# Linear attention stage: keys and queries of the next group ahead, expert weights of the preceding group on ScalarE

## The reference, cut to what matters

```
qkv = einsum('oc,bcn->bon', W_qkv, x_ext)   # x_ext: 256 tokens and 16 memory columns
q = softmax(q, over the 16 of a head) * SCALE
k = softmax(k, over the tokens and memory)
context = einsum('bhdn,bhen->bhde', k, v)
out = einsum('bhde,bhdn->bhen', context, q)
y = W_out @ out + b_out
y = (y - mean) / sqrt(var + EPS) * ln_g + ln_b
x = x + y
```

## Time and profile before

| what | value |
| --- | --- |
| median of 3 runs | 1226.85 us (1224.17 to 1227.85) |
| profiled execution | 1225.73 us, its span 1223.8 us |
| TensorE busy over the span | 913.3 us, 75% |
| VectorE busy over the span | 743.2 us, 61% |
| ScalarE busy over the span | 629.7 us, 51% |
| GpSimd busy over the span | 275.1 us, 22% |

### The profile page before, as it was taken

The page is one execution under the profiler, slowest core; times in us unless marked ns, Lnnn a source line. Parts: engine busy times, 40 slices in busy tenths (PEclk is TensorE's granted clock), DMA queues, the critical chain, the costliest instruction groups (busy, mean ns, idle before and its releaser), DMA issues. The chain is left out here.

```text
span 1223.8 us, 21857 instructions
## 1 busy us (share of the span) xinstructions
PE 913.3 (75%) x6760; PEld 593.2 (48%) x6760; DVE 743.2 (61%) x1939; ACT 629.7 (51%) x1286; POOL 275.1 (22%) x304
## 2 busy tenths in 40 slices
PE   4778426487878888075889895899675999977297
PEld 2566312377777778064666663333342333324142
DVE  6588769333333333576888887777587444445664
ACT  4444210133333333366888884687584777756253
POOL 2000110555656554232000001011231000015100
PEclk9565655699999899575999997899796999998699
DMA  3221160011010110200101110000100000000000
GB/s 110 66 59 47 32 109 0 19 20 21 18 19 19 19 19 12 80 35 10 53 35 51 51 44 18 1 1 0 53 1 1 1 1 0 0 0 21 1 0 35
DMA packets 25265, 33.05 MB, mean 27 GB/s; under 512 B 11376, under 2 KB 14422, under 8 KB 24814
## 3 DMA queue, kind: packets, MB, share of 16 engines
q1 hardware_dynamic: 20206, 27.50, 7.9%
q0 software_dynamic: 4992, 4.67, 2.0%
HBM read 19.31 MB, written 4.91 MB: 20 GB/s over the span
## 5 line engine op out<-in xcount | busy, mean ns | idle before, releaser
L1673 DVE SCALAR_TENSOR_TENSOR routed_hid_stage<-ps,routed_act_stage 128x512 f32<-128x512 f32 (+1 forms) x117 | 70.4, 602 | 176.7 <-ACT routed_act_stage L1457 139.5
L1746 PE MATMUL ps<-routed_x_stage,w_sb 128*128 128x256 f16 x858 | 122.6, 284 | 41.8 <-ACT routed_x_stage L1465 28.9
L1044 ACT ACTIVATE hid_stage<-ps,b_col_sb 128x512 f32<-128x512 f32 x192 | 122.8, 684 | 47.0 <-PE ps L985 46.8
L1457 ACT ACTIVATE routed_act_stage<-ps 128x512 f32<-128x512 f32 x117 | 70.3, 602 | 135.2 <-PE ps L1746 109.6
L1756 PE MATMUL ps<-w_sb,routed_hid_stage 128*128 x936 | 124.2, 276 | 3.7 <-issue 3.7
L1756 PEld LDWEIGHTS ps<-w_sb,routed_hid_stage 128*128 128x128 f32 x936 | 117.8, 197 | 5.7 <-issue 3.4
L1746 PEld LDWEIGHTS ps<-routed_x_stage,w_sb 128*128 x858 | 85.2, 104 | 60.0 <-issue 46.1
L985 PE MATMUL ps<-x_sb,w_sb 128*128 (+1 forms) x384 | 103.6, 388 | 6.1 <-ACT hid_stage L1044 6.1
L1002 PE MATMUL ps<-hid_stage,w_sb 128*64 128x512 f32 x384 | 105.2, 626 | 0.0
L1510 POOL DMA_INDIRECT routed_got_stage<-expert_rows,take_stage x78 | 80.3, 1029 | 81.7 <-DVE give_stage L1650 58.2
L1518 POOL DMA_INDIRECT expert_out<-routed_rows_stage,give_stage x78 | 78.2, 1002 | 89.9 <-ACT routed_rows_stage L1472 72.1
(11 more groups left out here) (382 smaller groups left out, 1878.4 us busy)
## 6 DMA issues: line engine op xcount, KB each, us to landing
w_stage_sb<-f_w SPq DMA_DIRECT2D x32, 176.0 KB, 3.1
x_sb<-w_sb SPq DMA_DIRECT2D x16, 256.0 KB, 2.4
rt_sb<-vals_stage SPq DMA_DIRECT2D x16, 256.0 KB, 2.3
rel_bias_sb<-bias_bands SPq DMA_DIRECT2D x16, 128.0 KB
w_stage_sb<-f_w SPq DMA_DIRECT2D x14, 128.0 KB, 3.0
w_sb<-f_w SPq DMA_DIRECT2D x1, 1536.0 KB
routed_got_stage<-expert_rows,take_stage POOLq DMA_INDIRECT x78
expert_out<-routed_rows_stage,give_stage POOLq DMA_INDIRECT x78
```

Source lines behind the costliest of these rows:

```text
L1044: nc.scalar.activation(hid[:, n % RING, :], ps[:, n % H_BANKS, :], func, bias=b1_col[:, b:b + 1], scale=UNSCALE).then_inc(h_act, 1)
L1457: nc.scalar.activation(act_h[:, n, :], ps[:, H1 + (q + n) % 2, :], ACT.Silu, scale=UNSCALE).then_inc(h_act, 1)
L1673: last = nc.vector.scalar_tensor_tensor(hid[:, q % 2, n, 0:full], ps[:, H3 + (q + n) % 2, 0:full], UNSCALE, act_h[:, n, 0:full], ALU.mult, ...
L1746: last = nc.tensor.matmul(o, w16[:, part, bass.ds(col, P)], xb[:, q % 2, :], start=(part == 0), stop=(part == 1))
```

## The change

TensorE makes k and q of group g+1 in one piece (`project(0)`, with a semaphore of its own, `queries_ps`), the values of g+1 behind the context in one piece (`project(1)`, `values_ps`), and turns the keys of g+1 (`turn_keys`) ahead of the last product of group g. VectorE takes maxima and subtraction of group g+1 at the head of group g, and so has q of g+1 ready in group g; it no longer copies the turned k, which ScalarE does (L602 of the changed kernel). ScalarE takes the square of group g-2 behind the exponential of q, and scales the weights of group g-1, one chunk behind the square and the other behind the x copy. In the LayerNorm, the bias `ln_b` is added to all of x at once by GpSimd at the head of the stage, the mean's factor is taken into the subtraction, and the multiplications by 1/sigma and `ln_g` become one instruction for each of the four tiles of 64 columns. The factor of the inverse sum goes into `mix`.

```
# ScalarE, group(g, squared=None, halves_of=None, last_group=False)
                         act.wait_ge(q_shifted, g + 1)
                         nc.scalar.activation(q_tok[:, :, :, :], q_tok[:, :, :, :], ACT.Exp,
                                              scale=UNSCALE).then_inc(q_exped, 1)
-                        act.wait_ge(qv_ps, g + 1)
+                        if squared is not None:
+                            square(squared)
+                        if halves_of is not None:
+                            split_high(halves_of, 0)
+                        act.wait_ge(values_ps, g + 1)
                         nc.scalar.activation(v_tok[:, :, :], v_ps, ACT.Copy, scale=UNSCALE).then_inc(v_copied, 1)
                         if not last_group:
                             nc.scalar.copy(x_grp[:, :], x16[:, bass.ds((g + 1) * GTOK, GTOK)]).then_inc(x_copied, 1)
-                        split_high(g, 0)
+                        if halves_of is not None:
+                            split_high(halves_of, 1)
                         act.wait_ge(kt_ps, g + 1)
                         nc.scalar.copy(kt_mem[:, :, :], ps[0:MEM, 4, 0:2 * HID0].rearrange(
-                            "p (b d) -> p b d", b=2)).then_inc(ktm_copied, 1)
-                        if not first:
-                            square(g - 1)
+                            "p (b d) -> p b d", b=2)).then_inc(kt_copied, 1)
+                        nc.scalar.copy(kt[:, :, :], ps[:, 3, :].rearrange(
+                            "p (t d) -> p t d", t=TPG)).then_inc(kt_copied, 1)
                         act.wait_ge(qt_ps, g + 1)
                         nc.scalar.copy(q_ch[:, :], ps[:, 7, :]).then_inc(qt_copied, 1)
-                        split_high(g, 1)
...
+                    group(0)
+                    group(1, halves_of=0)
+                    with act.Fori(2, GROUPS - 1) as g:
+                        group(g, squared=g - 2, halves_of=g - 1)
+                    group(GROUPS - 1, squared=GROUPS - 3, halves_of=GROUPS - 2, last_group=True)
+                    square(GROUPS - 2)
+                    split_high(GROUPS - 1, 0)
+                    split_high(GROUPS - 1, 1)
                     square(GROUPS - 1)
# TensorE
+                    def project(w):
+                        for t in range(TPG):
+                            for part in range(2):
+                                last = nc.tensor.matmul(qv[:, w, t, :], x_grp[:, t * P:(t + 1) * P],
+                                                        qvk16[:, part, w * HID0:(w + 1) * HID0],
+                                                        start=(part == 0), stop=(part == 1))
                         return last
...
# GpSimd
+                    pool.wait_ge(loaded["l0"], want["l0"])
+                    nc.gpsimd.tensor_tensor(x_tok[:, :, :], x_tok[:, :, :],
+                                            ln_rows[:, 2, :].unsqueeze(1).broadcast_to((P, NT, C)),
+                                            ALU.add).then_inc(x_biased, 1)
# VectorE, centre and finish
-                        c.link(nc.vector.tensor_scalar(y_st[:, 0, :], y_st[:, 0, :], 1.0 / C, None, ALU.mult))
-                        nc.vector.tensor_tensor(y, y, wide4(y_st[:, 0, :]), ALU.add).then_inc(y_sq_in, 1)
+                        nc.vector.scalar_tensor_tensor(y, wide4(y_st[:, 0, :]), 1.0 / C, y, ALU.mult,
+                                                       ALU.add).then_inc(y_sq_in, 1)
...
-                        c.link(nc.vector.tensor_tensor(y, y, wide4(y_st[:, 3, :]), ALU.mult))
-                        c.link(nc.vector.tensor_tensor(y, y, rows(1), ALU.mult))
-                        c.link(nc.vector.tensor_tensor(y, y, rows(2), ALU.add))
+                        for t in range(TPG):
+                            last = nc.vector.scalar_tensor_tensor(y[:, t, :], y[:, t, :], y_st[:, 3, t:t + 1],
+                                                                  ln_rows[:, 1, :], ALU.mult, ALU.mult)
+                        c.link(last)
# VectorE, group(g)
+                        if not last_group:
+                            maxima(g + 1)
                         if not first:
-                            variance(g - 1)
-                        split_low(g, 0)
-                        if not first:
-                            finish(g - 1)
+                            centre(g - 1)
+                        if not last_group:
+                            query_sums(g + 1)
                         dve.wait_ge(ctx_ps, g + 1)
                         nc.vector.tensor_tensor(ctx_t[:, :, :], ...
-                        split_low(g, 1)
+                        if not last_group:
+                            query_ready(g + 1)
                         dve.wait_ge(mix_ps, g + 1)
                         ...
+                        if not first:
+                            variance(g - 1)
+                        split_low(g, 0)
+                        if not last_group:
+                            dve.wait_ge(mix_ready, g + 1)
+                            key_inverse(g + 1)
+                        if not first:
+                            finish(g - 1)
+                        split_low(g, 1)
```

More of the change, by code:

```diff
@@ L576, in split_high, with group @@
                                              scale=WEIGHT_SCALE).then_inc(w_high_e, 1)
-                    def group(g, first=False, last_group=False):
+                    def group(g, squared=None, halves_of=None, last_group=False):
                         act.wait_ge(k_max, g + 1)
@@ L622, in keys, with turn_keys @@
                         last.then_inc(k_ps, 1)
-                    def queries_values(tiles):
-                        for t in tiles:
-                            for w in range(2):
-                                for part in range(2):
-                                    last = nc.tensor.matmul(qv[:, w, t, :], x_grp[:, t * P:(t + 1) * P],
-                                                            qvk16[:, part, w * HID0:(w + 1) * HID0],
-                                                            start=(part == 0), stop=(part == 1))
+                    def project(w):
[4 more added lines that the diff above has]
+                                                        start=(part == 0), stop=(part == 1))
                         return last
-                    def group(g, last_group=False):
+                    def turn_keys(g):
                         pe.wait_ge(k_exped, g + 1)
@@ L736, in split_low, with maxima @@
                                                        ALU.subtract).then_inc(w_split, 1)
-                    def group(g, first=False):
+                    def maxima(g):
                         dve.wait_ge(k_ps, g + 1)
@@ L780, in group @@
                             last = nc.vector.tensor_scalar(mix[:, b, :], ps[:, 6, b * C:(b + 1) * C],
-                                                           k_inv[:, b:b + 1], None, ALU.mult)
+                                                           k_inv[:, b:b + 1], DH0 ** -0.5, ALU.mult, ALU.mult)
                         last.then_inc(mix_ready, 1)
+                        if not first:
[7 more added lines that the diff above has]
+                        split_low(g, 1)
+                    maxima(0)
+                    query_sums(0)
+                    query_ready(0)
+                    key_inverse(0)
                     group(0, first=True)
-                    with dve.Fori(1, GROUPS) as g:
-                        c.loop(g, 15, start=1)
+                    dve.wait_ge(x_biased, 1)
+                    with dve.Fori(1, GROUPS - 1) as g:
+                        c.loop(g, 11, start=1)
                         group(g)
-                    c.end(GROUPS - 1)
+                    c.end(GROUPS - 2)
+                    group(GROUPS - 1, last_group=True)
                     for part in (centre, variance, finish):
```

36 lines of the change are left out of this document (17 added, 19 removed).

## The result

The changed kernel takes 1211.65 us (median of 4 runs, 1211.24 to 1213.31), the kernel before 1227.35 beside it: ratio 0.9871, 95% interval 0.9837 to 0.9905. It is 15.7 us faster. 1208.5 was forecast, in a range from 1202 to 1219. All medians and ratios here are those of fast runs; of the kernel before on the chip of experiments 5 to 8, two executions of 17, at 2808.1 and 4061.7 us, are left out for that.

The account below looks back on a forecast made before the run. VectorE's work was taken to bound the linear attention, plus waits for TensorE. Savings of 11.4 + 1.3 + 9.8 = 22.5 us, less 2.5 and 1.7, gave 18.3 off 1226.85: 1208.5 us, range 1202 to 1219.

Parts of the forecast that it names:

- VectorE sets the pace: Linear attention loop: VectorE's own work sets the group time, 10.25 us without waits, maxima of k 10.2 to 10.6 apart.
- What leaves VectorE: VectorE's groups: turned k's copy, two factors and the ln_b addition go, 1.43 us a group, 11.4 over 8.
- The four scale instructions: LayerNorm on VectorE: four 64-column instructions cost 0.91 us against 0.92 now, no difference taken; range -1.8 to +6.3 us.
- What stops waiting: VectorE's waits before the masked context and mix vanish, 9.8 us; less stretch over GpSimd's power, 1.3 us.
- The filling: Start of the stage: VectorE prepares two groups before the first context can be made, costing 2.5 us (1 to 5).
- GpSimd's addition costs nothing: Head of the stage: adding ln_b takes GpSimd 3.3 us, first awaited some 17 us after it began, so costs nothing.
- B: Linear attention: TensorE at 1.2 GHz becomes the bound, 11.2 us a group, 11.3 us gained, 1215.5 us; chance 0.22.
- D: Weight loads stall ScalarE ahead of the copy of v; landings of 6 us give 1212 us; chance 0.04.
- C: Linear attention: no wait remains and the filling is short, 2.0 us; 20.5 us gained, 1206.4 us; chance 0.13.
- E: GpSimd's ln_b addition is slow and VectorE waits at group 1; at 40 us long, 1231.5 us; chance 0.03.
- The sum: Whole kernel: 22.5 us gained, less 2.5 for filling and 1.7 in the loop, leaves 18.3 us; 1208.5 us.

Follow-up runs that it names:

- experiments 5 to 8: Four runs on one chip, where the kernel before takes 1161.5 us; the first repeats the changed kernel unaltered, ratio 0.9856 to the kernel before.
- experiment 3: The changed kernel with the copy of the turned k back on VectorE, behind the inverse of k; ratio 0.9918 to the kernel before.
- experiment 2: The changed kernel with ln_b added by VectorE once a group, without GpSimd's addition; ratio 0.9897 to the kernel before.
- experiment 4: The changed kernel's order on all engines with VectorE's arithmetic of the kernel before and no GpSimd addition; ratio 0.9924 to the kernel before.
- experiment 11: The changed kernel with GpSimd's addition in two halves, each waiting for a VectorE step, run a second time on another chip; ratio 0.9840 to the kernel before.
- experiment 7: The kernel before, in its own order, with only the changed arithmetic and ln_b added once by GpSimd; ratio 0.9974 to the kernel before.
- experiments 6 and 11: One kernel run on two chips: the changed kernel with GpSimd's addition in two halves, each waiting for a VectorE step; ratios 0.9839 and 0.9840 to the kernel before.
- experiment 8: The changed kernel with ScalarE scaling its own group's expert weights instead of the preceding group's; ratio 1.0224 to the kernel before.

## Why the prediction was right, and where it was off

- **VectorE sets the pace.** Right. 10.25 us a group without waits was worked out, 10.2 to 10.6 forecast, 10.38 measured. With one more copy on VectorE (experiment 3) a group grew by the length of that copy.
- **What leaves VectorE.** Right: the copy of the turned k, taken at 0.60, is 0.59 by experiment 3; `ln_b`, taken at 0.43, is 0.45 by experiment 2.
- **The four scale instructions.** 0.91 worked out from `mix`, 0.87 measured. The rule of the Trainium skill (VectorE: DVE Perf Modes, "The DRAIN you can't avoid") that the next instruction waits for an empty pipe would have made it 1.12; these rows do not bear it out.
- **What stops waiting.** Right: 9.8 became 2.2, by the order alone (2.9 in experiment 4). The order with the moved copy gives 9.3 us of the stage. The arithmetic gives 7.7 in the new order (experiments 4 and 11) and 2.6 in the old one (experiment 7).
- **The filling.** Too small: 2.5 was taken. VectorE's wait for the keys in the first three groups is 5.1 us, against 1.00 before. The second group costs 3 us more or less by the clock (experiments 6 and 11), and the forecast had no term for that.
- **GpSimd's addition costs nothing.** This is the step that failed. I had taken 3.3 us for its length and zero for its effect, with "if VectorE's two-input instructions stood still beside it, up to 3.3" as the bound. The addition took 4.49, as the Trainium skill's 4.5 (GPSIMD Engine Reference, "Elementwise — side-by-side cycle accounting") had it and not as the copy of 256 columns times eight, and held L709 for 3.84 more than it needs, which made the stage 3.4 to 3.9 longer. That this is so near the bound of 3.3 is chance: the bound was the length of an addition that was taken too short. I looked at when the result is first wanted, not at what else runs meanwhile; the first instruction of VectorE lies on the path of the stage. The stage was forecast at about 95 and came out at 99.4; without the hold it is 96.0 (experiment 11).
- **The rivals.** B did not come for the stage: from the third group on TensorE got the upper clock in part of each group (means of 0.79 to 0.84) and VectorE starts 10.38 apart. It came in the second group, where TensorE at the lower clock needed 10.7 and not the 11.2 worked out, so seven such groups would have cost less than B said. D's price is real (experiment 8); its slack was enough, except for the 1.3 us at the end. C did not come, as the filling was longer and not shorter. E's length was wrong, but its engine was the right one to look at.
- **The sum.** 18.3 forecast, 15.7 measured by the medians; the stage in the profile is only 13.6 shorter. Of the 4.7 that it lacks, 3.4 are the hold. The other 1.3 are a remainder of several terms: the filling cost more, a group a little less (10.38 against 10.25 + 0.25), and in the last group GpSimd's power took 1.58 instead of 1.01, with VectorE waiting for it. They were not separated by an experiment. The timed runs gained 2 us more than the stage did, which no run explains; the interval of the ratio (4 us to either side) allows for it. So that the number came out as near as 3 us is in part luck, while order, pace and waits came out as worked out.

The best version is that of experiments 6 and 11, with the addition in halves: ratios of 0.9839 and 0.9840 against 0.9871 and 0.9856 for the changed kernel. In each case it is the lower, by 0.2 to 0.3%, but the intervals overlap.

## What to carry to other kernels

Before you give GpSimd a long operation "beside" other work, look through VectorE's queue for that stretch: beside the additions and the copy of 2048 to 6144 columns here, each instruction that read two SBUF operands stood until the operation ended, even one of two columns, while one that reads PSUM and one SBUF operand (L764) and one that reads a single SBUF operand (L770) went on. Cut the operation and start its pieces where VectorE does one-operand or PSUM work. Economies on an engine pay in full only in an order in which nobody makes it wait: here the same arithmetic gave 2.6 us in the old order and 7.7 in the new one. And before a difference of 3 us between two profiles is put down to an edit, the groups are to be compared one by one: here one group at the other clock made as much.

## What the hardware showed

The hold was unexpected to me. L709 took 4.40 us instead of 0.56 beside an addition of 4.49, 13.02 beside one of 13.11, and 5.19 beside a copy of 5.30; a two-input instruction of two columns took 2.19 instead of 0.16. The Trainium skill says so (SBUF — State Buffer, "SBUF: two separate sides"): GpSimd and VectorE share a pair of ports under an exclusive lock for the whole instruction, and VectorE needs it for two SBUF inputs. By that rule the cost was to be had before the run, and these rows agree with it. In all of them GpSimd had started first.

Other rows show its limits. GpSimd's power on 4 columns, 1.01 us, has two operands in SBUF too, but VectorE's two-input split of 704 columns that began 0.02 behind it took 0.92 instead of 0.88: hardly any hold, and not one for the whole instruction. In the last group of the changed kernel it was the other way round: the split began first, at 123.28 (0.88 us), and the power, which began at 123.45, took 1.58. The same 1.58 stands in each profile that has the new order, so a hold of GpSimd by VectorE is the likely reading; no experiment was made on it.

GpSimd's rates per column were 2.2 ns for the addition of 2048 and 0.86 ns for the copy of 6144 columns.
